# Half-width absolute sums: the weight statistics of a fused attention and feed-forward layer, taken on VectorE in two steps per tile

## What is computed

```python
def ternary_quant(w):
    scale = jnp.mean(jnp.abs(w)) + EPS
    q = jnp.clip(jnp.round(w / scale), -1.0, 1.0) * scale
    return w + jax.lax.stop_gradient(q - w)
...
scores = jnp.einsum('bthd,bshd->bhts', q, k)
mask = jnp.tril(jnp.ones((T, T), dtype=scores.dtype))
scores = scores * mask
attn = jax.nn.softmax(scores / T ** 0.5, axis=-1)
...
x = x + _layernorm(_L0_attn_ref(_layernorm(x, axis=-1), Wq, Wk, Wv, Wo), axis=-1)
x = x + _layernorm(_L0_ffn_ref(_layernorm(x, axis=-1), W_up, W_gate, W_down), axis=-1)
```

## Time and profile before

| | us |
|---|---|
| median of the runs | 3333.45 |
| lowest and highest | 3330.82, 3336.09 |
| the profiled execution, its time | 3341.17 |
| its span on the slowest core (core 4) | 3339.6 |
| spans of all eight cores | 3290.7 to 3339.6 |

### The profile page before, as it was taken

One profiled execution on the slowest core, in us unless ns is written; L12 is line 12 of the kernel. 1 busy time (PEld: TensorE's weight loads), 2 busy tenths in 40 slices (PEclk: granted clock), 3 DMA queues, 4 the chain that ended last, 5 costly groups with the idle time before them and its releaser, 6 DMA issues.

```text
span 3339.6 us, 37142 instructions; the slowest of 8 cores (3290.7 to 3339.6 us)
## 1 busy us (share of the span) xinstructions
PE 2577.1 (77%) x12132; PEld 1259.0 (38%) x12132; DVE 1433.9 (43%) x1868; ACT 1100.9 (33%) x1221; POOL 313.9 (9%) x593
## 2 busy tenths in 40 slices
PE   3468967686786787976623999999999999999980
PEld 2333343352452443522212444444444444444430
DVE  4521144645645543321053535354444445453534
ACT  3443212213213123200035625344443525252602
POOL 1001020110110101001100101010110101010100
PEclk7567778887896888969965999999999999999995
DMA  4469765766667664013334626354453626261715
GB/s 132 135 183 251 209 155 193 238 178 232 202 183 253 183 194 114 4 25 40 44 112 155 213 85 190 113 163 141 137 166 108 188 88 196 83 212 60 210 36 164
DMA packets 136955, 498.19 MB, mean 149 GB/s; under 512 B 15728, under 2 KB 40304, under 8 KB 112192
## 3 DMA queue, kind: packets, MB, share of 16 engines
q1 hardware_dynamic: 54176, 297.89, 27.1%
q0 software_dynamic: 82592, 197.93, 23.4%
HBM read 512.46 MB, written 16.84 MB: 158 GB/s over the span
## 4 chain that ended last, share of the span: by engine, by line
PE 43%; DMA 20%; DVE 17%; issue 10%; ACT 9%; DVEq 0%; POOL 0%; ACTq 0%; POOLq 0%; SPq 0%
PE R L1586 43%; DMA arena_x<-GateL 8%; DVE arena_d L1586 5%; DVE arena_b L1586 4%; ACT qmC L1586 4%; DVE absP L1586 3%; DVE stripB L1586 2%; ACT stripA L1586 2%; ACT arena_d L1586 2%; DMA hbufB<-WoR 2%; DMA arena_x<-xs 2%; DMA arena_x<-xq 1%; DVE stats L1586 1%; DMA hbufA<-WoR 1%; DMA wqkD<-WqL 1%
## 5 line engine op out<-in xcount | busy, mean ns | idle before, releaser
L1586 PE MATMUL R<-arena_c,arena_d 128*128 128x512 bf16 (+3 forms) x4480 | 1024.4, 382 | 140.8 <-DVE arena_d L1586 49.0
L1586 PEld LDWEIGHTS R<-arena_c,arena_d 128*128 128x128 bf16 x4480 | 435.4, 99 | 714.4 <-issue 231.6
L1586 PE MATMUL R<-arena_b,arena_d 128*128 128x512 bf16 x2048 | 450.1, 383 | 16.9 <-DVE arena_d L1586 16.9
L1586 ACT ACTIVATE arena_d<-arena_x,s_up 128x1024 bf16<-128x1024 f32 x128 | 146.3, 1143 | 610.4 <-DVE arena_d L1586 601.5
L1586 DVE TENSOR_REDUCE absP<-arena_x 128x1 f32<-128x2048 f32 x128 | 292.0, 2281 | 123.4 <-DMA arena_x<-GateL 85.8
L1586 PEld LDWEIGHTS R<-arena_b,arena_d 128*128 128x128 bf16 x2048 | 201.5, 99 | 265.4 <-issue 29.4
L1586 ACT ACTIVATE stripA<-R 128x256 bf16<-128x256 f32 (+5 forms) x128 | 86.2, 673 | 493.6 <-PE R L1586 425.7
L1586 DVE CAST arena_d<-R 128x256 bf16<-128x256 f32 (+1 forms) x192 | 98.4, 512 | 337.9 <-PE R L1586 337.9
L1586 PE MATMUL R<-arena_d,arena_a 128*128 128x256 bf16 x2048 | 231.9, 278 | 12.5 <-DMA arena_d<-WvR 12.5
L1586 DVE TENSOR_TENSOR down_acc<-down_acc,R 128x2048 f32<-128x2048 f32 x56 | 128.1, 2287 | 233.0 <-PE R L1586 233.0
L1586 DVE TENSOR_TENSOR arena_d<-arena_d,qmC 128x1024 bf16<-128x1024 bf16 x128 | 88.6, 692 | 315.4 <-ACT qmC L1586 315.4
(11 more groups left out here) (159 smaller groups left out, 2701.1 us busy)
## 6 DMA issues: line engine op xcount, KB each, us to landing
arena_x<-DownR SPq DMA_DIRECT2D x64, 1024.0 KB, 6.9
arena_x<-UpL SPq DMA_DIRECT2D x64, 1024.0 KB, 5.6
arena_x<-GateL SPq DMA_DIRECT2D x64, 1024.0 KB, 5.6
arena_x<-UpL SPq DMA_DIRECT2D x128, 512.0 KB, 5.8
arena_x<-GateL POOLq DMA_DIRECT2D x128, 512.0 KB, 4.7
arena_x<-DownR POOLq DMA_DIRECT2D x128, 512.0 KB, 6.5
arena_d<-WvR POOLq DMA_DIRECT2D x128, 64.0 KB, 6.9
arena_x<-xs SPq DMA_DIRECT2D x11, 512.0 KB, 4.5
```

Of the source, the lines that this page charges most:

```text
L1586: ins = getattr(eng, m)(*a, **k)
```

## The change

VectorE's list now has 256 entries in place of 128: each tile of UpL and GateL appears twice, as half 0 and half 1. A slot takes one entry. For half 0 SyncE loads the whole tile as before, and VectorE sums the absolute values of columns 0 to 1023 into a spare column of `absP` (number 64 of the matrix' block). For half 1, in the next slot, VectorE sums columns 1024 to 2047 into the tile's own column, waits for that, and adds the spare column to it. Only then, before that addition, is the buffer counted as read. The number of slots and their places are unchanged, and the tiles on ScalarE are as before.

```diff
-        abs_sched_dve = [(wi, ec) for ec in range(p.EC) for wi in (0, 1)]
+        abs_sched_dve = [(wi, ec, half) for ec in range(p.EC)
+                         for wi in (0, 1) for half in (0, 1)]
...
-                dma_in("sync", buf, buf.ap[:, :], src[ec])
                 if wi < 2:
-                    @sec("vector")
-                    def _(v2, w, buf=buf, col=col):
-                        buf.rd(w)
-                        tk = eV.inc(v2.reduce_sum(absP.ap[:, col:col + 1],
-                                                  buf.ap[:, :], axis=AX.X,
-                                                  apply_absolute_value=True))
-                        buf.note_read(tk)
-                        absP.note_write(tk)
+                    if half == 0:
+                        abs_state["next"] += 1
+                        buf = xtA if i % 2 == 0 else xtB
+                        abs_state["dve_buf"] = buf
+                        hD2 = p.D // 2
+                        dma_in("sync", buf, buf.ap[:, :], src[ec])
+                        tcol = wi * 72 + 64
...
+                            tk = eV.inc(v2.reduce_sum(
+                                absP.ap[:, tcol:tcol + 1],
+                                buf.ap[:, 0:hD2], axis=AX.X,
+                                apply_absolute_value=True))
+                            absP.note_write(tk)
+                            buf.note_read(tk)
+                    else:
+                        buf = abs_state["dve_buf"]
...
+                            t1 = eV.inc(v2.reduce_sum(
+                                absP.ap[:, col:col + 1],
+                                buf.ap[:, hD2:2 * hD2], axis=AX.X,
+                                apply_absolute_value=True))
+                            buf.note_read(t1)
+                            w.wait(t1)
+                            tk = eV.inc(v2.tensor_add(
+                                absP.ap[:, col:col + 1],
+                                absP.ap[:, col:col + 1],
+                                absP.ap[:, tcol:tcol + 1]))
+                            absP.note_write(tk)
```

More of the change, by code:

```diff
@@ L647, in emit_abs @@
             for _ in range(n):
+                half = None
                 if which in ("act", "any") and \
@@ L652, in emit_abs @@
                 elif abs_state["next_dve"] < len(abs_sched_dve):
-                    wi, ec = abs_sched_dve[abs_state["next_dve"]]
+                    wi, ec, half = abs_sched_dve[abs_state["next_dve"]]
                     abs_state["next_dve"] += 1
@@ L660, in emit_abs, with _ @@
                 i = abs_state["next"]
-                abs_state["next"] += 1
                 src = (UpL, GateL, DownR)[wi]
-                buf = xtA if i % 2 == 0 else xtB
                 col = wi * 72 + ec
-                dma_in("sync", buf, buf.ap[:, :], src[ec])
                 if wi < 2:
-                    @sec("vector")
-                    def _(v2, w, buf=buf, col=col):
-                        buf.rd(w)
-                        tk = eV.inc(v2.reduce_sum(absP.ap[:, col:col + 1],
-                                                  buf.ap[:, :], axis=AX.X,
-                                                  apply_absolute_value=True))
-                        buf.note_read(tk)
-                        absP.note_write(tk)
-                else:
+                    if half == 0:
[5 more added lines that the diff above has]
+                        tcol = wi * 72 + 64
+                        @sec("vector")
+                        def _(v2, w, buf=buf, tcol=tcol, hD2=hD2):
+                            buf.rd(w)
+                            tk = eV.inc(v2.reduce_sum(
[6 more added lines that the diff above has]
+                        buf = abs_state["dve_buf"]
+                        hD2 = p.D // 2
+                        tcol = wi * 72 + 64
+                        @sec("vector")
+                        def _(v2, w, buf=buf, col=col, tcol=tcol, hD2=hD2):
+                            buf.rd(w)
+                            t1 = eV.inc(v2.reduce_sum(
[9 more added lines that the diff above has]
+                            absP.note_write(tk)
+                else:
+                    abs_state["next"] += 1
+                    buf = xtA if i % 2 == 0 else xtB
+                    dma_in("sync", buf, buf.ap[:, :], src[ec])
```

## The result

The changed kernel takes 1.0117 times the time of before (95% interval 1.009 to 1.0144). On the median of 3333.45 us shown before that is 3372 us; its undisturbed executions took 3358.67, 3375.73 and 3376.10 us. (Many executions of any kernel here were longer with the cores of one die at a lower clock; all ratios leave them out, and of e2's profile only cores 4 to 7 are read.) The forecast was 3378 us.

The account below looks back on a forecast made before the run. Heads were taken as bound by a two-buffer loop of tile loads, projections by TensorE. Drain +187, heads -141 and projections -1 gave +45 us: 3386 us profiled, 3378 us for the median (+1.3%), range 3330 to 3435.

Parts of the forecast that it names:

- The drain: After the last scaling: 48 whole tiles left, loaded through two buffers at 7.85 us per two tiles, a loss of 187 us.
- The heads: Eight pairs of heads: 47.7 us a pair, 382 us against 522.8, a gain of 141 us.
- Narrow chunks: Last four slots of a head: 8.7 us in sum, 3.0 us more than without tiles.
- three terms of the head: Charges per head over the pair without tiles: 0.3 us wide chunks, 3.0 us narrow chunks, 0.8 us waiting for a tile.
- the tile waits: Narrow slots at a head's end: 0.8 us waited per head; at the start of a pair, 2 us per pair.
- the wide halves: First half of a head: half a reduction hides behind matmuls, with 0.3 us a head charged for the wait.
- The additions: 128 additions with waits: 0.35 us in every second slot of a head; if all hidden, 1 us shorter per head.
- The projections: Seven stretches between pairs: bound by TensorE, reductions stay hidden, 59.8 us each, a gain of 1 us.
- A: Slower rival: heads keep waiting for tiles, 53 us a pair, +87 us, 3420 us; chance 0.26.
- B: Rival without loss: drain nearer the bandwidth (158 us), heads don't wait, +2 us, 3336 us; chance 0.12.
- C: Rival: heads don't speed up, held near 71 us a pair by something else, +232 us, 3565 us; chance 0.02.
- The clock: Pairs of heads: granted clock expected between 0.70 (with tiles) and 0.91 (without), nothing charged for it.

Follow-up runs that it names:

- e2: Changed kernel with both halves of a tile and the addition in one slot, in V projection and heads: 1.0032 times the kernel before.
- e8: The changed kernel measured again, on the same chip as other kernels of that call: 1.0112 times the kernel before.
- e7: Changed kernel without the 128 additions, each half summing into its own column: 1.0117 times the kernel before.
- e6: As e4, but 3 tiles per head, and the 16 left over go one behind each scaling, with four buffers: 0.9581 times the kernel before.
- e1: Kernel before, whole tiles, with an empty entry after each tile of VectorE's list, so every second slot is used: 1.0074 times the kernel before.
- e4: Kernel before, whole tiles, VectorE's 16 per group spread 2 in K projection, 6 in V projection, 4 per head: 0.9617 times the kernel before.
- e10: As e6, with four buffers in the first four groups, 2 tiles per head there, 1 in the others, more in projections: 0.949 times the kernel before.

## Why the prediction was right, step by step

The time, the sign and the mechanism were right: the same loads and reductions, only later, with a stretch at the end that nothing else fills. That the number came within 6 us is partly luck, since its terms missed in opposite directions. On core 4 the heads gained 10 us more than forecast, the drain was 2 us shorter, the projections were 5 us worse, and the scalings, to which I charged nothing, took 2 us more; on the average of the cores the heads gained 161 us, 20 more than forecast.

- **The drain.** 187 us forecast; 185.4 to 189.6 on six cores, 203 on two, and much the same in e8. The loop was worked out from the second heads of before and held: 7.8 us per turn on average where 7.85 was said. Not foreseen was the pair of neighbours.
- **The heads.** 47.7 us a pair forecast, 43.5 to 48.5 measured, 360 to 372 us for all eight against 382. The gain on core 4 is 151 us where 141 was said. Narrow chunks: from the mask of the ninth chunk to the row sum I said 8.7 us. Core 1, second head of its second pair, VectorE's timeline:

```profile
577.28 0.28 DVE L1617 TENSOR_TENSOR R<-R,arena_d 128x128 f32<-128x128 f32 x1
...
589.16 0.30 DVE L1617 TENSOR_TENSOR R<-R,arena_d 128x128 f32<-128x128 f32 x1 [0.19 <-PE R L1617]
...
597.64 1.21 DVE L1617 TENSOR_TENSOR den_f<-R,counts_b 1x1024 f32<-1x1024 f32 x1 [1.08 <-PE R L1617]
```

8.48 us (589.16 to 597.64), 0.18 us of tile wait in it. All three terms of the head were somewhat too large. Over both heads of this pair the narrow ends cost 4.8 us beyond tile waits (6.0 forecast), the tile waits 2.8 us (3.6: the first head waited 0.65, 1.33 and 0.59 us, this one 0.18), and the wide halves cost nothing where I charged 0.6: this one took 11.88 us (577.28 to 589.16), 0.7 less than without tiles.
- **The additions.** "Were it hidden in all of them, the heads would be 1 us shorter per head" failed: e7 took them away and nothing came back, since the tile wait behind them grew by as much. The prediction's own terms say so. Its tile wait of 0.8 us was worked out with 0.35 us of addition in two of the three slots; without them it would be 1.5 us. Only in the eighth pair, beside which no K or V weights load, did about 1.6 us come back for two heads, where I had said 2.
- **The projections.** 59.8 us each forecast, 60.5 measured; not 1 us gained but 4 lost. I had read "busy, hence unaffected". A projection can start at the lower clock without being any less busy, as the windows under e6 show. Before, six of the seven projections were slow already (60.3 us on average); now the last one is too (57.9 to 60.5 us), and it accounts for 2.7 of the 4 us. That the reductions at the end of the heads cause it fits e6 and is not settled by e1.
- **A slip in the text.** The four ScalarE tiles in the seventh pair are not in that pair's last slots but in the last four slots of its first head (SyncE issues them from 1274.17 to 1286.7 us, in a pair that runs from 1259.50 to 1316.29). No term rests on it.
- **The rivals.** A (heads wait for tiles throughout) did not happen, pairs were nowhere near 53 us. B (a drain at the bandwidth) did not happen with two buffers and did with four. C is out.

The clock in the pairs of core 4 came out between the two values, 0.80 to 0.87, as said. Left open: why one pair of neighbouring cores drains at 4.2 us per tile. On core 1 the loads come unevenly: for most of the drain one is issued 2.5 to 3.4 us behind the one before, and the next 4.8 to 6.5 us later. Both take over 6 us, but whether this comes from the memory that the pair shares was not tried on fewer cores.

## What to carry to other kernels

Work that fills gaps is a budget of slots times size: halve the size without adding slots, and the rest lands at the first place that needs the result, where nothing covers it. Before splitting a filler to unburden a stage, look for the stage whose windows show spare time on the DMA engines and on the engine that does the work, and move it there; here that alone was worth 3.8% (e4), and 5.1% with more buffers (e10), while halving lost 1. And when windows show a stage waiting for loads well under the full DMA share, count the buffers before blaming the bandwidth: two gave 264 GB/s in the drain, four 338.

## What was not expected of the hardware

- One pair of neighbouring cores, another one in each of four profiles, drained two-buffered 1 MB loads at 238 to 244 GB/s (loads of 5.9 to 6.3 us) while the others had 256 to 266 (5.1 to 5.4 us). With four buffers all eight cores took the same 145 to 146.5 us.
- TensorE can start a dense stage at the lower of its two clock levels, which its busy share hides: 13.6 busy us did 53 matmuls at a granted 0.82 (changed kernel) or 65 at 1.00 (e6), and in one profile with the same work ahead of both, 54 at 0.83 or 64 at 1.00 (e1). In e1 the pair of heads behind a projection at full clock was 2.2 us longer, so the 2.8 us saved there were mostly lost again.
